# LayerNorm transposes, two next-turn score blocks and a high part, put at other places in one hand-written order

## What is computed

```python
h = _layernorm(x) * (1 + ca) + sa
x = x + ga * attention(h, weight_qkv, weight_proj)   # causal, softmax
h = _layernorm(x) * (1 + cb) + sb
x = x + gb * ffn(h, ...)                             # gated, Hadamard-rotated weights
```

## Time and profile before

| | us |
|---|---|
| median of 3 runs | 946.15 (945.91 to 946.38) |
| the profiled execution | 946.18 |
| its span, first to last instruction | 944.2 |
| TensorE busy | 918.9 |
| VectorE busy | 639.2 |
| ScalarE busy | 507.1 |
| GpSimd busy | 461.9 |

### The profile page before, as it was taken

One profiled execution on the slowest core, in us unless ns is written; L12 is line 12 of the kernel. 1 busy time (PEld: TensorE's weight loads), 2 busy tenths in 40 slices (PEclk: granted clock), 3 DMA queues, 4 the chain that ended last, 5 costly groups with the idle time before them and its releaser, 6 DMA issues.

```text
span 944.2 us, 15025 instructions
## 1 busy us (share of the span) xinstructions
PE 918.9 (97%) x5504; PEld 811.5 (86%) x5504; DVE 639.2 (68%) x1312; ACT 507.1 (54%) x1102; POOL 461.9 (49%) x679
## 2 busy tenths in 40 slices
PE   5989999999999999999999999999999999999997
PEld 4878888888888888888888888888888897888886
DVE  6567757764787578647875787478757876864554
ACT  3366656654766476647664766476647665321111
POOL 2366718570767176707671867076717684120000
PEclk9989999999999999999999999999999999999999
DMA  7000100000001000000010000000001011000000
GB/s 278 23 1 1 41 1 23 1 28 1 23 1 40 1 23 1 28 1 23 2 40 1 23 1 29 2 22 2 1 1 45 1 57 46 1 18 6 22 22 22
DMA packets 10181, 21.34 MB, mean 23 GB/s; under 512 B 1281, under 2 KB 5633, under 8 KB 9985
## 3 DMA queue, kind: packets, MB, share of 16 engines
q1 hardware_dynamic: 9392, 20.24, 6.3%
q10 hardware_dynamic: 720, 0.21, 0.1%
HBM read 18.35 MB, written 2.10 MB: 22 GB/s over the span
## 4 chain that ended last, share of the span: by engine, by line
PE 77%; DVE 13%; ACT 7%; issue 2%; POOL 0%; DMA 0%; DVEq 0%; SPq 0%; ACTq 0%; POOLq 0%
PE ps L1055 17%; PE ps L1057 17%; PE ps L1056 17%; PE ps L1189 9%; DVE ps L949 5%; PE ps L1178 5%; PE ps L1175 5%; PE ps L1172 5%; ACT prob L704 4%; DVE pt_lo L953 3%; ACT pt_hi L729 2%; PE ps L1079 1%; DVE xhat L827 1%; DVE stats L811 1%; DVE vare L819 1%
## 5 line engine op out<-in xcount | busy, mean ns | idle before, releaser
L576 POOL TENSOR_TENSOR rinv<-rsum,mone 128x1 f32<-128x1 f32 x256 | 144.9, 566 | 252.2 <-ACT prob L704 252.0
L953 DVE TENSOR_TENSOR pt_lo<-ps,pt_hi 128x512 fp32r<-128x512 f32 x288 | 198.1, 688 | 64.7 <-ACT pt_hi L729 61.5
L729 ACT ACTIVATE pt_hi<-ps 128x512 fp32r<-128x512 f32 x288 | 171.2, 597 | 124.4 <-PE ps L1189 124.1
L704 ACT ACTIVATE prob<-ps,nmax 128x256 f32<-128x256 f32 (+28 forms) x256 | 180.8, 706 | 85.2 <-DVE nmax L949 84.2
L949 DVE CUSTOM_DVE_ANT_0 ps<-ps,mask_f 128x256 f32<-128x256 f32 (+28 forms) x256 | 182.6, 719 | 47.4 <-PE ps L1178 45.3
L581 POOL TENSOR_SCALAR prob<-prob,rinv 128x256 f32<-128x256 f32 (+28 forms) x256 | 183.6, 717 | 38.2 <-POOL rinv L576 38.2
L1189 PE MATMUL ps<-ident,prob 128*128 128x128 f32 x1152 | 173.0, 273 | 1.9 <-POOL prob L581 1.5
L1189 PEld LDWEIGHTS ps<-ident,prob 128*128 128x128 f32 x1152 | 141.2, 141 | 20.5 <-DVE pt_lo L953 2.1
L1055 PE MATMUL ps<-pt_hi,v_hi 128*128 128x512 f32 x288 | 134.5, 467 | 2.1 <-DVE pt_lo L953 2.1
L1057 PE MATMUL ps<-pt_hi,v_lo 128*128 128x512 f32 x288 | 113.7, 395 | 0.0
L1056 PE MATMUL ps<-pt_lo,v_hi 128*128 128x512 f32 x288 | 113.5, 394 | 0.0
(11 more groups left out here) (149 smaller groups left out, 1783.9 us busy)
## 6 DMA issues: line engine op xcount, KB each, us to landing
w_raw<-in_wqkv SPq DMA_DIRECT2D x8, 640.0 KB, 4.1
wp_raw<-in_wproj SPq DMA_DIRECT2D x8, 512.0 KB, 3.4
prob<-in_wug SPq DMA_DIRECT2D x4, 512.0 KB, 4.6
out_y<-prob SPq DMA_DIRECT2D x8, 256.0 KB, 2.2
x<-in_x SPq DMA_DIRECT2D x3, 512.0 KB, 12.2
prob<-in_wmod SPq DMA_DIRECT2D x1, 1024.0 KB, 9.4
wv_raw<-in_wv SPq DMA_DIRECT2D x4, 256.0 KB, 4.6
raw_down<-in_wdn SPq DMA_DIRECT2D x1, 1024.0 KB, 4.7
```

Source lines behind the costliest of these rows:

```text
L704: a_.activation(row(i, h).rearrange("p (a n) -> p a n", a=nb), score_banks(i, h).rearrange("p (a n) -> p a n", a=nb)[:, :, 0:w], ACT.Exp, ...
L729: a_.activation(pt_hi[:, n % 3, :], ring(t, "T", n), ACT.Copy).then_inc(pth_done, 1)
L953: v_.tensor_tensor(pt_lo[:, n % 3, :], ring(t, "T", n), pt_hi[:, n % 3, :].bitcast(F32), ALU.subtract).then_inc(ptl_done, 1)
```

## The change

- Items L are taken out of the filling around a T and stand behind the value product that follows it: `T14 V12 L S2.2 T15`.
- In turns 1 to 7 LF moves to the first window. It is alone in `fill[4]` there, so it stands ahead of T4: `T3 V1 LF T4 V2`. In turn 0 it stays.
- S0.1 and S0.2 of the next turn stand behind V35: `T35 V33 V34 V35 S0.1 S0.2 Y3`.
- ScalarE takes no exponentials at T34 and at S0.0 of a next turn. Those of S7.3 and S0.0 come behind pt_hi(35).

```diff
+            if p == (t == 0):
+                fill[0 if p else 4].append((t, "LF", 0, 0))
             if p == 1:
-                for k, what in ((0, "LF"), (3, "LN"), (5, "L"), (6, "LH"), (7, "LL")):
+                for k, what in ((3, "LN"), (5, "L"), (6, "LH"), (7, "LL")):
                     fill[k].append((t, what, 0, 0))
...
             for n, extra in zip(units, fill):
+                transposes = [item for item in extra if item[1] == "L"]
+                extra = [item for item in extra if item[1] != "L"]
                 out += extra[:1] + [(t, "T", n, 0)] + extra[1:]
                 behind.append(n)
                 if len(behind) > LAG:
                     value()
+                out += transposes
         while behind:
-            if len(behind) == LAG and t + 1 < TURNS:
-                value()
-                out += scores(t + 1, 0)[1:3]
             value()
+        out += scores(t + 1, 0)[1:3] if t + 1 < TURNS else []
...
                 if what == "S":
-                    exps()
+                    if not (t and n == h == 0):
+                        exps()
                     waiting.append((t, n, h))
                 if what == "T":
                     act.wait_ge(t_done, this(t_done, t, n + 1))
                     a_.activation(pt_hi[:, n % 3, :], ring(t, "T", n), ACT.Copy).then_inc(pth_done, 1)
-                    exps()
+                    if n != NU - 2:
+                        exps()
```

## The result

The changed kernel takes 948.81 us (median of 18 runs, 947.86 to 949.78) against 946.45 us for the kernel before in the same rounds (18 runs): a ratio of 1.0026, 95% interval [1.0019, 1.0033]. It is slower by about 2.4 us; 2.0 had been forecast. The profiled execution took 947.89 us, with a span of 945.9.

The account below looks back on a forecast made before the run. The prediction took the kernel as TensorE-bound, busy 97% of the span, with order changes only adding or removing holds. Its terms, -3.8 - 2.5 + 5.5 + 2.8 = +2.0 us, gave 948.2 us, range 943.0 to 950.5.

Parts of the forecast that it names:

- Part 1: LayerNorm transposes L behind V12, eight turns: T14 to T15 shrinks from 2.56 to 2.07 us, 3.8 us gained in all.
- part 2: Statistics LF moved ahead of T4, turns 1 to 7: 2.5 us gained at S5.3, 5.5 us lost at T6.
- Part 2, the gain: Second window, turns 1 to 7: S5.3 no longer held behind the statistics, 0.35 us a turn, 2.5 us.
- L's hold: Wait of transposes L for VectorE's pt_lo(13) after T14; either move would remove it, counted once, in Part 1.
- Part 2, the cost: First window: vare held by GpSimd's scaling, so pt_lo(4) and T6 come 0.78 us later, 5.5 us over seven turns.
- Rival 1: vare issues ahead of GpSimd's scaling or isn't held: cost 0.08 instead of 0.78 a turn, 943.3 us; chance 0.15.
- Part 3: End of turn, seven boundaries: V35 earlier, but Y3 later because o_hi(3) queues behind both exponentials; 2.8 us lost.
- the held first product: Y3's first product runs longer after its wait, bringing the loss per boundary from 0.38 to 0.4 us.
- V35's gain: End of turn: pt_hi(35) ahead of the exponentials lets V35 start 0.68 us earlier.
- Rival 2: Y3 is not held, o_hi(3) coming earlier: each boundary gains 0.23 instead of losing 0.4, 943.8 us; chance 0.15.
- Rival 3: Late queue after Y3 holds S6.0 and S6.2: 3.2 us more over seven boundaries, 951.4 us; chance 0.10.
- margins of 0.1: Slack in us for S6.0 and S6.2 after Y3 before a VectorE or ScalarE slip would hold them.

Follow-up runs that it names:

- e1: Kernel before with only the LayerNorm transposes L moved behind V12 in all eight turns: 943.81 us against 946.62, ratio 0.9972.
- e2: Kernel before with only the statistics LF moved ahead of T4 in turns 1 to 7: 946.18 us against 946.62, ratio 0.9998.
- e3: Kernel before with only the end-of-turn edits, S0.1 and S0.2 behind V35 and ScalarE's exponentials behind pt_hi(35): 949.77 us against 946.62, ratio 1.0036.
- e4: Changed kernel, but in turns 1 to 7 GpSimd waits for vare before scaling S6.2's row: 943.21 us against 946.62 before, ratio 0.9967.
- e6: Kernel before with only ScalarE's exponentials of S7.3 and S0.0 moved behind pt_hi(35): 949.22 us against 946.32, ratio 1.003.
- e5: Kernel before with only S0.1 and S0.2 moved behind V35, ScalarE's order kept: 953.78 us against 946.32, ratio 1.0076.
- e7: Changed kernel with the old end of turn and LF ahead of T8 in turns 1 to 7: 940.36 us against 946.32 before, ratio 0.9935.

## Why the prediction was right, step by step

- **Part 1** was summed at -0.49 a turn and -0.34 in turn 0; the trace has -0.50 and -0.39. T15 just fitted in turns 1 to 7, as worked out, and only because part 2 had made ScalarE and VectorE earlier: e1, without part 2, gains 0.37 instead. T15 of turn 0 was held for 0.13; 0.15 had been forecast.
- **Part 2, the gain**: 0.35 forecast, 0.37 measured, and e2 confirms that L's hold would have gone with it. The two parts therefore share a gain: e1 -2.8, e2 -0.4 and e3 +3.1 add up to -0.1, the whole change has +2.4, and 2.2 of the difference is L's hold counted twice (7 x (0.37 + 0.44 - 0.50)). Counting it once was a step of the sum that mattered as much as any price.
- **Part 2, the cost**: 0.78 forecast, 0.75 to 0.80 measured. The step on which all hung was to take vare as held by GpSimd's scaling; e4 shows it, and the price: 4.80 instead of 5.52 to 5.55 between T4 and T7, 5.2 us in seven turns (5.6 between the medians) against 4.9 summed. The Trainium skill, "SBUF — State Buffer", section "Who interferes with whom", has the rule of an exclusive port that goes to the first to issue; the trace (0.91 with the scaling issued 0.11 ahead, 0.17 without it) agrees as far as the scaling comes first; no run here has vare first and a scaling right behind it. The scaling was forecast to lead by 0.13 and led by 0.09 to 0.12 in the seven turns. Rival 1 did not happen, but a margin that small is in part luck: some 5 us, and the sign of the result, hung on it.
- **Part 3**: Y3 was forecast 0.38 later, which made 0.4 with the held first product; the trace has 0.38 and 0.04 for that product, so that the seven boundaries, with turn 1's own excess, cost 3.0 us and not 2.8. V35's gain was forecast at 0.68 and is 0.67. Rival 2 is out by e3 and e6. TensorE's wait ahead of Y3 begins at 335.60 (335.24 + 0.36), 0.1 earlier than I had it, since the two small blocks take 0.36 and not 0.45; nothing hung on it.
- **Rival 3** stayed away in six of seven boundaries. Behind turn 1, where VectorE has one more instruction at T34 (a step of `gate_down`), pt_lo(35) is late, V35 starts 2.36 behind T35 instead of 2.05, and Y3 to Y4 is 2.98 instead of 2.84 and the way to the next T1 0.1 longer. I had noted margins of 0.1; they were used up once. e5 shows what happens when they are gone everywhere: 0.67 more at each boundary, beside the 0.36 of the blocks themselves. e6, with the blocks ahead of V35, doesn't lose it even behind turn 1.
- **The size**: 2.0 us forecast, 2.4 measured between medians, 2.1 by the starts of the two traces. By starts each term came out as summed, within 0.2 us: -3.9, -2.6, +5.5 and +3.0 against -3.8, -2.5, +5.5 and +2.8. The net is smaller than each of them, and rival 1 or rival 2 alone would have turned its sign. The forecast lay at the 0.2% that I had called the bound of what can be told from no change; the interval of the measured ratio begins at 0.19%.

## What to carry to other kernels

Where one engine is busy all the time, price a change of order by the starts of its instructions around each moved item, and for each wait that goes away work out what the next instruction in the queue needs; here V35 came 0.67 us earlier and the work behind it 0.38 later, because ScalarE's order had been turned around in front of something else that was wanted. A small instruction can be dear where another engine waits for what stands behind it, and what runs beside it on another engine counts too: the same statistics cost 0.8 us a turn ahead of T4 beside a GpSimd scaling, 0.04 there without it, and nothing ahead of T8. Parts that remove the same hold must be counted together: each alone gains, the sum does not.

## What the runs showed of the hardware

- A VectorE `TENSOR_SCALAR` on two columns took 0.17 us alone and 0.90 to 0.92 us beside a GpSimd `TENSOR_SCALAR` that had started 0.09 to 0.12 us before it. In the kernel before, at the old place, it took 0.71 or 0.72 with the scaling started 0.13 to 0.15 ahead, and 0.59 in turn 4, where it had started 0.27 ahead. In all these cases its end followed the end of the scaling by 0.01 to 0.03 us, so that its length was what was left of the scaling. The two `BATCH_NORM_STATS2` ahead of it, one input each, took 0.74 together in the changed kernel and in e4, and 0.75 in e7, where a scaling of 0.48 us ran beside them (262.72, above). In e7 a GpSimd `TENSOR_TENSOR` on one column, issued 0.04 us behind vare, did not lengthen it.
- One order in one queue decided about more than its own items: moving two score blocks of 0.36 us together cost 7.5 us with one order of ScalarE's queue (e5) and some 0.2 with the other (e3 beside e6, by starts).
